# Zeros and repack on SyncE's queue, 60 maxima ahead of the picked experts, and decays from three bf16 parts

## The reference

```python
x = L0_attn_x
xn = _layernorm(x, axis=-1)
s = _L0_attn_ref(xn, ...)            # softmax(q k^T / sqrt(8), causal) v, then wo
g = _silu(_L0_ffn_ref(xn, ...))      # top 4 of 32 experts
x = x + s * g
xn = _layernorm(x, axis=-1)
s = _L1_attn_ref(xn, ...)            # gated delta rule
g = _silu(_L1_ffn_ref(xn, ...))      # top 2 of 8 experts
x = x + s * g
```

```python
def step(S, xs):
    qt, kt, vt, gt, bt = xs
    S = S * jnp.exp(gt)[..., None, None]
    kS = jnp.einsum('bhk,bhkv->bhv', kt, S)
    S = S + bt[..., None, None] * kt[..., :, None] * (vt - kS)[..., None, :]
    o = jnp.einsum('bhk,bhkv->bhv', qt, S)
    return (S, o)
```

## Time and profile before

| what | value |
|---|---|
| runs shown | 2314.37, 2314.36, 2313.28 us, median 2314.36 us |
| profiled execution | 2313.63 us; its span 2311.6 us, granted clock 0.962 of full speed |
| PE | 2015.2 us busy, 87% of the span |
| DVE | 1538.9 us, 67% |
| ACT | 982.5 us, 43% |
| POOL | 758.4 us, 33% |
| DMA | 107.37 MB, mean 46 GB/s |

### The profile page before, as it was taken

One profiled execution on the slowest core, in us unless ns is written; L12 is line 12 of the kernel. 1 busy time (PEld: TensorE's weight loads), 2 busy tenths in 40 slices (PEclk: granted clock), 3 DMA queues, 4 the chain that ended last, 5 costly groups with the idle time before them and its releaser, 6 DMA issues.

```text
span 2311.6 us, 39665 instructions
## 1 busy us (share of the span) xinstructions
PE 2015.2 (87%) x13026; PEld 1516.7 (66%) x13066; DVE 1538.9 (67%) x2459; ACT 982.5 (43%) x2529; POOL 758.4 (33%) x685
## 2 busy tenths in 40 slices
PE   4578888884588599999999999999999999999996
PEld 2257643334344387878778778787787787877875
DVE  3968841124555577777777777777777777777775
ACT  1012247761010345545445355454454544545544
POOL 4630011102000415336154262361542524615332
PEclk8889989996799799999999999999999999999998
DMA  7446630000011000000000000000000000000001
GB/s 264 147 153 197 196 103 27 18 1 23 23 32 44 25 33 28 14 32 27 9 27 14 32 27 14 23 20 25 27 14 32 27 13 24 18 27 27 14 23 37
DMA packets 72034, 107.37 MB, mean 46 GB/s; under 512 B 22918, under 2 KB 54934, under 8 KB 68790
## 3 DMA queue, kind: packets, MB, share of 16 engines
q1 hardware_dynamic: 64446, 86.60, 12.0%
q10 hardware_dynamic: 4478, 11.88, 1.4%
q0 software_dynamic: 3072, 8.39, 1.1%
HBM read 81.48 MB, written 28.52 MB: 48 GB/s over the span
## 4 chain that ended last, share of the span: by engine, by line
PE 48%; DVE 13%; ACT 3%; issue 3%; POOL 0%; DMA 0%; DVEq 0%; ACTq 0%; POOLq 0%
PE ps L1430 6%; PE ps L1558 5%; PE ps L1550 5%; PE ps L1468 4%; PE ps L1478 3%; DVE P L1961 3%; DVE P_term L1958 3%; DVE conv L1882 3%; PE ps L1615 3%; PE ps L1493 2%; PE ps L1604 2%; PE ps L1564 2%; PE ps L1504 2%; PE ps L1617 2%; PE ps L1591 2%
## 5 line engine op out<-in xcount | busy, mean ns | idle before, releaser
L1882 DVE SCALAR_TENSOR_TENSOR conv<-raw,tap_st,conv 128x1024 f32<-128x1024 f32 x204 | 299.9, 1470 | 3.8
L1430 PE MATMUL ps<-xnT,w_conv_st 128*128 128x512 f32 x544 | 250.4, 599 | 4.4 <-DMA w_conv_st<-in_w_conv 4.4
L1862 POOL TENSOR_TENSOR o<-o,silu_z 128x256 f32<-128x256 f32 x128 | 138.3, 1080 | 255.7 <-DVE silu_z L1902 141.7
L824 DVE TENSOR_REDUCE m_part<-ps 128x1 f32<-128x640 f32 (+7 forms) x176 | 175.1, 1026 | 49.1 <-PE ps L675 32.7
L1756 POOL TENSOR_TENSOR gmask_Q<-upto,g 128x2048 f32<-128x2048 f32 x17 | 61.4, 3610 | 433.7 <-PE ps L1571 433.6
L1635 ACT COPY raw<-ps 128x512 f32<-128x512 f32 x136 | 80.7, 594 | 271.3 <-PE ps L1430 271.3
L990 ACT ACTIVATE probs<-ps 128x1024 f32<-128x1024 f32 (+7 forms) x256 | 146.0, 660 | 44.5 <-PE ps L940 24.1
L1430 PEld LDWEIGHTS ps<-xnT,w_conv_st 128*128 128x128 f32 x544 | 97.7, 191 | 97.2 <-issue 88.6
L1842 POOL TENSOR_TENSOR kq_decayed<-conv,decay_rows 128x1024 f32<-128x1024 f32 x64 | 158.3, 2504 | 0.0
L1478 PE MATMUL ps<-w_z_st,xnT 128*128 128x256 f32 x512 | 148.8, 393 | 0.0
L1468 PE MATMUL ps<-w_out_st,xn_nat 128*128 128x256 f32 x544 | 126.2, 386 | 0.7
(11 more groups left out here) (340 smaller groups left out, 4741.7 us busy)
## 6 DMA issues: line engine op xcount, KB each, us to landing
decay_rows<-scratch_egc SPq DMA_DIRECT2D x17, 1024.0 KB, 4.7
w_conv_st<-in_w_conv SPq DMA_DIRECT2D x17, 512.0 KB, 3.3
scratch_slots_x<-yacc ACTq DMA_DIRECT2D x8, 1024.0 KB, 10.2
slot_rows<-scratch_slots_x SPq DMA_DIRECT2D x16, 512.0 KB, 5.0
scratch_slots_y<-slot_outputs SPq DMA_DIRECT2D x16, 512.0 KB, 3.8
w_gate_up<-in_gu SPq DMA_DIRECT2D x8, 768.0 KB, 8.0
w_gate_up<-in_gu SPq DMA_DIRECT2D x32, 192.0 KB, 3.1
w_out_st<-in_w_out SPq DMA_DIRECT2D x17, 256.0 KB, 2.6
```

Source lines behind the costliest of these rows:

```text
L824: dve.tensor_reduce(dst, src, AX.X, ALU.max).then_inc(s_max, 1)
L1430: mm = pe.matmul(ps[:, 6 + n % 2, :], wc[:, k, (n // 2) * P:(n // 2 + 1) * P], m.xnT[:, k, (n % 2) * HALF:(n % 2 + 1) * HALF], start=k == ...
L1862: g.tensor_tensor(oc, oc, zs[:, c, :], ALU.mult).then_inc(s_oz, 1)
L1882: op = dve.scalar_tensor_tensor(out=cv[:, t, :], in0=raw[:, t, at:at + T], scalar=tap[:, t, at:at + 1], in1=cv[:, t, :], op0=ALU.mult, op1 ...
```

## The change

Four edits are in it.

1. The zero-fill and the repack go from ACT's queue to SP's. The zeros stand behind SP's four input loads and wait only for the tile of zeros; the repack stands behind the loads of the first stacks, at the end of the stage.
2. In the next stage SP loads stacks 1 and 2 before it waits for the repack and loads the first weights.
3. `FIRST_OP` goes from 52 to 60 and `first_op(g)` to `60 + 7g + (g + 3) // 4`: 60 maxima precede step 0, and 116 instead of 124 stand in and behind the 16 steps.
4. `g` is split into three bf16 parts (five small DVE operations in `stage_l1_inputs`). `gmask` becomes three POOL operations of 128x2048 with bf16 output, one a part. Two of the results fill the space of `gm_q`, the third lies in `X`, and since `X` is read until PE L1580 ends, `gmask` now waits for that line's results and not for L1571's. D becomes three bf16 matmuls a bank in place of one in f32.

```diff
@@ stage_inputs, SP
             sp.dma_start(m.w_o[:], w_o.rearrange("(k p) n -> p k n", p=P)).then_inc(in_wo, 16)
+            sp.wait_ge(s_clear, 1)
+            for i in range(SLOTS // T):
+                sp.dma_start(m.slots_x[T * i:T * (i + 1), :].rearrange("(p a) d -> p (a d)", p=P),
+                             m.yacc[:].rearrange("p c d -> p (c d)")).then_inc(m.s_zeroed, 16)
...
             load_stacks(sp, m, 0)
+            for i in range(E0 // G0):
+                sp.dma_start(m.down_rows[G0 * i:G0 * (i + 1)].rearrange("g f d -> (g f) d").rearrange("(t p) d -> p t d", p=P),
+                             down0[i].rearrange("p (t d) -> p t d", d=D)).then_inc(m.s_rows, 16)
@@ stage_inputs, ACT
-            act.wait_ge(s_clear, 1)
-            act.wait_ge(in_x, 16)
-            act.wait_ge(in_w, 32)
-            for i in range(SLOTS // T):
-                act.dma_start(m.slots_x[...], m.yacc[...]).then_inc(m.s_zeroed, 16)
-            for i in range(E0 // G0):
-                act.dma_start(m.down_rows[...], down0[i]...).then_inc(m.s_rows, 16)
@@
-FIRST_OP = 52
+FIRST_OP = 60
...
-    return FIRST_OP + g * 8 - g // 4
+    return FIRST_OP + g * 7 + (g + 3) // 4
@@ stage_maxima_and_moe0, SP
+            load_stacks(sp, m, 1)
+            load_stacks(sp, m, 2)
             sp.wait_ge(m.s_rows, 16 * (E0 // G0))
             for g in range(2):
                 load_weights(g, g)
-            for group in range(1, 5):
-                if group == 4:
-                    sp.wait_ge(s_sc, 1)
-                load_stacks(sp, m, group)
+            load_stacks(sp, m, 3)
+            sp.wait_ge(s_sc, 1)
+            load_stacks(sp, m, 4)
@@ stage_l1_inputs, DVE
+            dve.wait_ge(s_g, 1)
+            step(dve.tensor_copy(m.afterb[:], m.after[:]))
+            step.link(dve.tensor_copy(m.g3[:, 0], m.g[:]))
+            step.link(dve.tensor_tensor(g_rest[:], m.g[:], m.g3[:, 0], ALU.subtract))
+            step.link(dve.tensor_copy(m.g3[:, 1], g_rest[:]))
+            step.link(dve.tensor_tensor(m.g3[:, 2], g_rest[:], m.g3[:, 1], ALU.subtract))
@@ stage_delta, PE
-                pe.wait_ge(s_gm, i + 1)
+                pe.wait_ge(s_gm, i * 3 + 3)
...
-                    pe.matmul(ps[:, b, :], m.after[:], chunks(gm_q[:, b // 2, 4 * (b % 2):4 * (b % 2) + 4, :]),
-                              start=True, stop=False)
+                    for part in range(3):
+                        pe.matmul(ps[:, b, :], m.afterb[:], gm_part(part)[:, b * HALF:(b + 1) * HALF], start=part == 0, stop=False)
@@ stage_delta, POOL
             def gmask(r):
-                gsrc = m.g[:, 0:2, :] if isinstance(r, int) else m.g[:, bass.ds(2 * r, 2), :]
-                g.tensor_tensor(gm_q[:], m.upto[:].unsqueeze(1).unsqueeze(1).broadcast_to([P, 2, NC, P]),
-                                gsrc.unsqueeze(3).broadcast_to([P, 2, NC, P]), ALU.mult).then_inc(s_gm, 1)
+                for part in range(3):
+                    gsrc = m.g3[:, part, 0:2, :] if isinstance(r, int) else m.g3[:, part, bass.ds(2 * r, 2), :]
+                    g.tensor_tensor(gm_part(part).rearrange("p (e c i) -> p e c i", e=2, c=NC),
+                                    m.upto[:].unsqueeze(1).unsqueeze(1).broadcast_to([P, 2, NC, P]),
+                                    gsrc.unsqueeze(3).broadcast_to([P, 2, NC, P]), ALU.mult).then_inc(s_gm, 1)
...
-                pool.wait_ge(s_x, i * ND + ND)
+                pool.wait_ge(s_y, i * ND + ND)
                 gmask(i + 1)
```

More of the change, by code:

```diff
@@ L205, in build @@
         m.g = sb("g", [P, NV + 2, NC])
+        m.g3 = sb("g_parts", [P, 3, NV + 2, NC], BF16)
+        m.afterb = sb("after_bf", [P, P], BF16)
         m.eg = sb("decays", [P, 3, NV + 2, NC])
@@ L467, in _ @@
         def _(act):
-            act.wait_ge(s_clear, 1)
-            act.wait_ge(in_x, 16)
-            act.wait_ge(in_w, 32)
-            for i in range(SLOTS // T):
-                act.dma_start(m.slots_x[T * i:T * (i + 1), :].rearrange("(p a) d -> p (a d)", p=P),
-                              m.yacc[:].rearrange("p c d -> p (c d)")).then_inc(m.s_zeroed, 16)
-            for i in range(E0 // G0):
-                act.dma_start(m.down_rows[G0 * i:G0 * (i + 1)].rearrange("g f d -> (g f) d").rearrange("(t p) d -> p t d", p=P),
-                              down0[i].rearrange("p (t d) -> p t d", d=D)).then_inc(m.s_rows, 16)
             for k in range(KT):
@@ L1062, in stage_l1_inputs @@
         egT = sb("egc_turned", [P, 2, P])
+        g_rest = sb("g_rest", [P, NV + 2, NC])
         in_w = sem("small_in")
@@ L1386, in two_banks, with gm_part @@
             return ps[:, b:b + 2, :].rearrange("p b n -> p (b n)")
+        def gm_part(part):
+            if part < 2:
+                return chunks(gm_q[:].rearrange("p e c i -> p (e c) i")).bitcast(BF16)[:, part * 2 * T:(part + 1) * 2 * T]
+            return chunks(xs[:].rearrange("p e c i -> p (e c) i")).bitcast(BF16)
         SU_BANK = (2, 0)
```

## The result

The changed kernel takes 2352.23 us (median of 4 runs, 2349.08 to 2356.61), the kernel before 2313.82 (4 runs, 2310.39 to 2314.37): ratio 1.0166, 95% interval 1.0146 to 1.0186. It is slower by 38 us. The profiled execution took 2353.62 us.

The account below looks back on a forecast made before the run. PE was taken to set the delta loop's pace, with ACT's DMA issues delaying PE at the front. Terms -13.4 (front) - 5.3 (maxima) + 0 + 12.5 (gmask) = -6.2 gave 2308 us, range 2292 to 2351.

Parts of the forecast that it names:

- rival (b): Delta loop: gmask's first part runs before `conv` B, first copy of S late, +3.4 x 16 = +54 us, 2350; chance 0.24.
- DVE first: Delta loop: `conv` B starts 0.01 us before gmask and runs undisturbed; later waits cost +0.78 x 16 = +12.5 us.
- gmask at 3.6 us: POOL in the delta loop: each bf16 gmask part takes 3.6 us, 10.8 in all, 7.2 more an iteration.
- (a): Delta loop: `conv` B goes before gmask, update of S 0.78 us late an iteration, +12.5 in all, 2308; chance 0.50.
- D at 0: Delta loop: three bf16 matmuls a bank end PE's D 0.85 us sooner an iteration, costed at nothing; whole bound -13.6.
- POOL's own time as no bound in itself: Delta loop: POOL can spare gmask's 7.2 us more an iteration, being busy 38.55 of 93; the price is DVE's delay.
- The lock: DVE and POOL, delta loop: whoever starts first keeps the other out for its whole length; DVE operations reading PSUM not held.
- Edit 1: Front: without ACT's 16 DMA issues PE starts projections 12.5 us earlier, L435 2.2 shorter; next stage at 55.6, gain 13.4.
- Edits 2 and 3: Maxima stage: +7.7 - 6.4 - 6.6 = -5.3 us, between -2.5 and -9.
- eight more maxima ahead of step 0: Maxima stage: eight more maxima alone before the steps cost 8 x 0.96 = +7.7 us.
- the first wait for rows: Maxima stage, ahead of step 0: the stall for the load of rows goes, 6.6 us gained, between 4.7 and 10.1.
- eight fewer stand among the steps: Maxima stage: eight fewer maxima among the steps, 0.8 us each, give -6.4, with bounds of 0.5 and 0.96 each.

## Why the prediction was wrong

The range ended at 2351, and 2352.23 was measured; the direction given the most weight was the wrong one. The kernel went the way of rival (b), to which the prediction gave 0.24. That (b)'s 2350 lies near is in part luck: it holds a gain of 18.7 for the front and the maxima stage, of which 11.4 came, and +54 for the loop, of which 51.4 came. The range's upper end took (b) with that whole gain, though the prediction's own bounds for it went down to 6.0 and 2.5.

**The step that failed** is "it starts at 1230.15 ... `conv` B starts 0.04 later, at 1230.14 ... DVE first". The times were right, the verdict was not. In the trace after, in the iteration shown, `conv` B's record starts at 1230.889 and gmask's at 1230.908: DVE leads by 0.02 us, about as worked out (0.01), in all sixteen iterations (0.019 to 0.026), and POOL goes first every time (`conv` B takes 4.70 us). So 0.02 us between the starts of two records do not tell which of the two goes first. Nor is it chance: another pair, with the same lead, ends the other way in all sixteen iterations (0.017 to 0.032). DVE and POOL near the end of the loop:

```profile
1256.99 1.23 DVE L1926 TENSOR_TENSOR o<-o,o_rsqrt 128x1024 f32<-128x1024 f32 x1
```
```profile
1257.02 1.78 POOL L1878 TENSOR_TENSOR o<-o,silu_z 128x256 f32<-128x256 f32 x1
```

Here DVE takes its own 1.23 and POOL waits (1.78; the same product takes 0.73 alone). This pair is in the trace before too (1252.86 and 1252.89, 1.23 and 1.78) and spoke for DVE; in the earlier trace rows DVE led by 0.18. Nothing in that trace showed that the `conv` operation, a scalar_tensor_tensor, loses with such a lead, and what makes the two pairs differ no run here tells. A lead of 0.01 us that was worked out from the times of other instructions should have weighed about the same on both sides. The run with a product ahead of gmask shows that the order decides: 96.35 against 93.62 us, by which of the two is first.

**What was right.** gmask at 3.6 us (3604 ns). The price of each case: (a) 0.78 predicted, 0.64 measured; (b) 3.4 predicted, 3.37 measured. D at 0: 92.97 against 92.98 measured. POOL's own time as no bound in itself: right for three long parts, wrong for 24 short ones. The lock, for a whole instruction: `conv` B takes 4.70 us in place of 1.28, across the 3.60 of gmask's first part, and the earlier start decided at a distance of 0.18 us, but not at 0.02. That DVE's operations that read PSUM are not held: in the kernel after the 32 updates of S that lie wholly inside a product of gmask (as the one at 1240.31, inside the third, 1239.02 to 1243.07) take 342 to 349 ns, and the 160 others 339 to 348; the 32 copies of o inside take 408 to 425, the 96 clear of any 418 to 427. What the two engines share no run shows: "the port" in rival (b) and in the expectations is a word for this lock. That L1946 is long by what POOL does beside it: 0.42 us at 812.05, where no `kq_decayed` runs, against 2.46.

**What was missed in (b).** Behind PE's wait of 1.9 us for the first copy of S the clock can fall, to 0.59 over 4.2 us (its records hold 0.50 and 1.00 and nothing between). In the changed kernel it does so in 6 of 16 iterations and changed no sum, since parts 1 and 2 of gmask hold the updates back by as much, but with a single late gmask it is 1.64 us of 3.41 in every second iteration.

**Edit 1**: -13.4 predicted, -11.9 measured. The terms: the late load of x 0.9, which brings PE to 24.62 against 23.7 with the wait for `xnT` as forecast, and L435 1.9 longer than taken. With both the chain worked out to end at 54.3 ends at 57.1, and the next stage starts at 57.2. The premise that failed is that PE comes to L435 at the full pace. The repack's issues took 0.85 us each, hidden, against 1.15.

**Edits 2 and 3**: -5.3 predicted, +0.5 measured on the first chip. Of the three terms, two hold about: eight more maxima ahead of step 0 take 6.9 us (the 52nd ends at 108.75, the 60th at 115.68; predicted 7.7), and the first wait for rows is gone: step 0 starts 10.3 us earlier on a stage that starts 11.9 earlier, 1.6 later from the stage's start in spite of these 6.9. The term that failed is "eight fewer stand among the steps ... -6.4". The waits of DVE in the stage after, and PE's matmuls that turn the rows (first and last start):

```profile
DVE m_part L825 <- PE ps L676: 39.0, 54, 6.0
```
```profile
L687 PE MATMUL ps<-ident,slot_rows x128: 272/273/477, 114.2 to 289.8; 128*128 128x128 f32 x128
```

From the first row turned to the last it is 175.6 us here, and was 175.9 (124.4 to 300.3); what follows up to the attention is 0.9 shorter. So the -6.4 came to -1.2. The steps took as long with seven maxima between them as with eight, and the time of those left out became DVE's idle time: ahead of all maxima this was 49.1 us, 10.13 of it the stall that is gone, and is 50.7 (both by the pages; the 39.0 above are a part, 32.7 before). A part is the second wait for rows, which the prediction took to stay: PE waits 3.7 us for it at 156.8 before and 5.1 at 145.6 now. What else sets the pace of the steps stays open.

## What to carry to other kernels

When a long operation moves beside another that it can hold up, as gmask did `conv` B (4.70 us for 1.28), work out both orders, and weigh them about equally unless the starts lie clearly apart (here 0.17 us decided by the start, 0.02 to 0.03 did not): which is first can cost more than the work, and a cheap operation put ahead can decide it. Before you explain a loop by one iteration, look at the others: here the low clock stood in the one shown and not in most. Cut long operations of the less urgent engine into pieces and give them a head start, so that they are done before the next thing that waits for that engine (92.76 us an iteration here, against 96.35). Work that is hidden behind other work gives back nothing when it is taken out, as D's 0.85 us and the maxima among the steps did: look for what ends last there before counting it.

## What was not expected of the hardware

- Two instructions of DVE and POOL whose records start 0.02 us apart: the one with the later record went first, in all sixteen iterations of the kernel after and of the run with the late f32 gmask (4.70 and 4.71 us for 1.28), while another pair with a lead of 0.02 to 0.03 went by the start of the record (1.23 and 1.78 us).
- Behind the same wait of PE, 1.92 us at the same place of the program, the granted clock falls in every second iteration from the third on (0.59 over 4.2 us) with one late gmask, and in 6 of 16 in the kernel after (there 1.91 us), and not in the others.
- On some chips PE's and DVE's pace halves while POOL issues indirect DMAs (132 matmuls and 71 in the same 38 us), with PE waiting in part (14.4 us from 57 to 150 us) for nothing that the profile shows.
